# Eight-expert stages: the bias rows computed during the first blocks instead of after the last one

## The chip, the cores and the metric

The kernel runs on one core of a Trainium2 chip. The metric is the device time of one execution in microseconds, lower is better. Several executions are timed, and one further execution is recorded by the profiler. That execution has a time of its own, and its span runs from its first to its last instruction.

## The reference, cut to what matters

1,024 tokens of width 256 pass six stages, each added to a running `x`: a two-expert feed-forward, attention, the two-expert feed-forward again, an eight-expert feed-forward, a state-space mixer, the eight-expert feed-forward again. Each stage begins with a layernorm. The eight-expert stage is the one that changes. It is called twice, as the fourth and as the last stage, with the same weights:

```
logits = gelu(x @ rw1) @ rw2;  wgt, idx = top_k(softmax(logits), 2)
for e in range(8):
    Ye = gelu(x @ w1[e] + b1[e]) @ w2[e] + b2[e]
    Ce = gelu(b1[e]) @ w2[e] + b2[e]
    for k in range(2):
        mask = idx[..., k] == e
        active = any(mask)
        out = out + active * wgt[..., k] * where(mask, Ye, Ce)
x = x + 0.5 * out
```

So every token gets, besides the outputs of its own two experts, a sum of constant rows: for every active expert that it did not choose the row `Ce`, and for the chosen ones the row `b2[e]`, each weighted. This sum of constants is what is called the bias rows here: a matrix of coefficients (1,024 tokens by 16) times a matrix of 16 rows (8 of `Ce`, 8 of `b2`) by 256.

## The kernel before, in words

All activations live in SBUF as `X`, eight tiles of 128 tokens by 256. Each engine (PE for matmuls, ACT, DVE, POOL, SP for queueing transfers) runs its own instruction list in order and meets the others at semaphores. PSUM has eight banks of 512 f32 columns, `c.bank(0)` to `c.bank(7)`.

An eight-expert stage (`moe_stage` with `gated` false) goes like this. Layernorm, router and sorting give lists of token indices, so that the tokens of one expert stand in blocks of 128; there are 23 blocks (`NB`). Per block:

- POOL issues `slab_in` (line 935: 1 MB of first-layer weights of the block's expert into one of four slabs), `gather` (line 954: the block's tokens) and, once the block is done, `scatter` (line 959: its 128 output rows to `y_dram`). Its order is fixed: `slab_in(b+4)`, `gather(b+4)`, `scatter(b)`.
- PE transposes the gathered tokens (`turn_x`, line 545, bank 7), runs the first layer (`first_turned`, line 572, 48 f16 matmuls of 128 columns, banks 0 to 3) and the second layer (`second`, line 602, 24 f16 matmuls of 256 columns, bank 6). In `step_turned(b)` the order is `turn_x(b+2)`, `first_turned(b+1)`, `second(b)`.
- ACT copies the transposed tokens (line 682) and applies gelu (line 695).
- DVE makes the low halves (lines 837, 854 and 856; the last two in `half_h`) and copies the output out of PSUM (`block_y`, line 863).

Behind the last `second` stands the bias work. PE turns the coefficients `coef` (16 columns) with 8 f32 products into banks 2 and 3 (line 653). In the first of the two stages it also turns the rows `Ce` (`bias_turn`, line 1055, bank 7), to which DVE adds `b2` (`bias_add`, line 1065). ACT copies the turned coefficients to SBUF (line 740). PE multiplies them with the 16 rows, one f32 product of 256 columns for each tile of tokens (line 661, banks 0, 1, 4, 5). DVE adds half of each to `X` (line 912). In the trace each f32 product is two matmul instructions.

SP waits until all scatters have landed and then queues eight loads of 256 KB (line 985), each of which fetches a token tile's two expert rows. In `combine_first` (line 920) and `combine_second` (line 925) DVE adds them with their weights to `X`. `combine_first` of a tile waits for that tile's load and for that tile's bias row (`s_bts`). After the first of the two stages the combines run inside the mixer's layernorm, in which PE also runs unused matmuls (`keep_awake`, line 114); after the second each finished tile is stored.

Of the kernel before, what the change touches and what calls it, by code (L numbers as in the profile page):

```python
# [19 lines left out]
P = 128  # L20
T = 1024
D = 256
# [300 lines left out]
def moe_stage(c, src, E, TOPK, NB, gated, W, region, meanwhile=None, weights_act=None, weights_dve=None, weights_late=None, weights_sync=None):  # L323
# [154 lines left out]
    def pe(eng):  # L478
# [108 lines left out]
        def second(b, p, first_use=False):  # L587

            e = eng.value_load(ebi[0:1, bass.ds(b, 1)], min_val=0, max_val=E - 1)
            if not first_use:  # L590
                eng.wait_ge(*s_yo(b))
            else:
                for ready in W["second_ready"]:
                    eng.wait_ge(*ready)
            w2h, w2l = W["second"]
            i = 0
            for q in range(2):
                eng.wait_ge(*s_hl(2 * b + q + 1))
                for j in range(half):
                    at = bass.ds(e * (CF * D) + (q * half + j) * D, D)  # L600
                    for a, w in ((hTh, w2h), (hTh, w2l), (hTl, w2h)):
                        ins = eng.matmul(c.bank(6)[:, 0:D], a[:, 0 if gated else p, q * half + j, :], w[:, at],  # L602
                                         start=(i == 0), stop=(i == 3 * CF - 1))
                        i += 1
            ins.then_inc(s_y.sem, 1)

        if not gated:

            eng.wait_ge(*s_yi(1))
            W["bias_wait"](eng)  # L610
        for ready in W["block_ready"]:
            eng.wait_ge(*ready)
        def step(b, p, first_use=False, x=True):
# [4 lines left out]
                turn_x(b + 2, p)  # L618
            second(b, p, first_use)

        def step_turned(b, p, q, first_use=False, x=True):

            if x:
                turn_x(b + 2, p)
            first_turned(b + 1, 1 - p, (q + 1) % SLABS, first_use)
            second(b, p, first_use)

        turn_x(0, 0)
        turn_x(1, 1)
        if gated:  # L630
            first(0, 0)
            step(0, 0, True)
            step(1, 1)
            with eng.Fori(1, NB // 2 - 1) as i:
                step(2 * i, 0)
                step(2 * i + 1, 1)
            step(NB - 3, 0)
            step(NB - 2, 1, x=False)
            turn_h(NB - 1, 0)
        else:  # L640
            first_turned(0, 0, 0, True)
            step_turned(0, 0, 0, True)
            step_turned(1, 1, 1)
            with eng.Fori(0, NB // 4 - 1) as i:
                for j in range(2, 6):
                    step_turned(4 * i + j, j % 2, j % SLABS)
            for b in range(NB - 5, NB - 1):
                step_turned(b, b % 2, b % SLABS, x=(b < NB - 2))
        second(NB - 1, 0)
        if not gated:  # L650
            eng.wait_ge(*s_cf(1))
            for t in range(NT):
                ins = eng.matmul(c.bank(2 + t // 4)[0:2 * E, (t % 4) * P:(t % 4 + 1) * P], coef[:, t, :], c.ident[:, :],
                                 start=True, stop=True)
            ins.then_inc(s_cft.sem, 1)
            W["bias_turn"](eng)
            eng.wait_ge(*s_cfc(2))
            for ready in W["bias_done"]:
                eng.wait_ge(*ready)
            for t in range(NT):  # L660
                eng.matmul(c.bank((0, 1, 4, 5)[t // 2])[:, t % 2 * D:(t % 2 + 1) * D], coefT[:, t * P:(t + 1) * P], W["cb"], start=True, stop=True)\
                    .then_inc(s_bt.sem, 1)

    assert NB % 2 == 1 and (gated or NB % SLABS == 3)

# [1 line left out]
    def act(eng):  # L667
        L["act"](eng)
        if not gated:
            for s in range(HALVES):  # L670
                eng.wait_ge(*s_hid(s + 1))
                eng.activation(hid[:, s * BANK:(s + 1) * BANK], c.bank(s), ACT.Gelu).then_inc(s_hida.sem, 1)
        eng.wait_ge(*s_d(1))
        eng.activation(ex[:, :, :], lg[:, :, :], ACT.Exp).then_inc(s_ex.sem, 1)
        if weights_act is None:
            eng.activation(c.spent[:, 1:2], c.ln_consts[:, 0:1], ACT.Silu if gated else ACT.Gelu)
        if weights_act is not None:
            weights_act(eng)

        def block_x(b, p):  # L680
            eng.wait_ge(*s_xt(b + 1))
            eng.activation(xgh[:, p, :, :], c.bank(7)[:, 0:D].rearrange("p (k t) -> p k t", k=KD), ACT.Copy).then_inc(s_xh.sem, 1)  # L682

        def block_act(b, p):
            eng.wait_ge(*s_h1(b + 1))
            eng.activation(h[:, p, :], c.banks(0, 2), ACT.Silu).then_inc(s_a.sem, 1)  # L686

        def block_gelu(b, p, s, first_use=False):

            if not first_use:  # L690
                eng.wait_ge(*s_hl(2 * b - 2))
            for q in range(2):
                eng.wait_ge(*s_h1(2 * b + q + 1))
                for j in range(q * CF // 2, (q + 1) * CF // 2):
                    ins = eng.activation(h[:, p, j * P:(j + 1) * P], c.banks(2 * p, 2)[:, j * P:(j + 1) * P], ACT.Gelu,  # L695
                                         bias=slabs[s][:, KD * FF + j:KD * FF + j + 1])
                ins.then_inc(s_h.sem, 1)

        def block_h(b, p):
            for q in range(2):  # L700
                eng.wait_ge(*s_ht(2 * b + q + 1))
                eng.activation(hTh[:, 0, q * 4:q * 4 + 4, :], c.bank(4 + q).rearrange("p (j t) -> p j t", j=4), ACT.Copy)\
# [12 lines left out]
        def step_turned(b, p, s, first_use=False, x=True):  # L715
            if x:
                block_x(b + 2, p)
            block_gelu(b + 1, 1 - p, (s + 1) % SLABS, first_use)

        block_x(0, 0)  # L720
        block_x(1, 1)
        if gated:
            block_act(0, 0)
            for b in range(NB - 3):
                step(b, b % 2)
            step(NB - 3, 0)
            step(NB - 2, 1, x=False)
            block_h(NB - 1, 0)
        else:
            block_gelu(0, 0, 0, True)  # L730
            step_turned(0, 0, 0, True)
            step_turned(1, 1, 1)
            with eng.Fori(0, NB // 4 - 1) as i:
                for j in range(2, 6):
                    step_turned(4 * i + j, j % 2, j % SLABS)
            for b in range(NB - 5, NB - 1):
                step_turned(b, b % 2, b % SLABS, x=(b < NB - 2))
            eng.wait_ge(*s_cft(1))
            for s in range(HALVES):
                eng.activation(coefT[:, s * BANK:(s + 1) * BANK], c.bank(2 + s)[0:2 * E, :], ACT.Copy).then_inc(s_cfc.sem, 1)  # L740


    def dve(eng):
# [121 lines left out]
        def step(b, p, first_use=False, x=True):  # L865
# [7 lines left out]
            if meanwhile is not None:  # L873
                meanwhile["dve"](eng, b, True)

        def step_turned(b, p, first_use=False, x=True, y=True):
            if y:
                block_y(b - 1, 1 - p, first_use)
            if x:
                block_x(b + 2, p)  # L880
            half_h(b + 1, 1 - p, 0)
            half_h(b + 1, 1 - p, 1)
# [12 lines left out]
        else:  # L895
            half_h(0, 0, 0)
            half_h(0, 0, 1)
            step_turned(0, 0, y=False)
            step_turned(1, 1, True)
            step_turned(2, 0, True)  # L900
            with eng.Fori(1, NB // 2 - 1) as i:
                step_turned(2 * i + 1, 1)
                step_turned(2 * i + 2, 0)
            step_turned(NB - 2, 1, x=False)
            block_y(NB - 2, 1)
        block_y(NB - 1, 0)

        if not gated:
            W["bias_add"](eng)
            for t in range(NT):  # L910
                eng.wait_ge(*s_bt(t // 2 * 2 + 2))
                eng.scalar_tensor_tensor(c.X[:, t, :], c.bank((0, 1, 4, 5)[t // 2])[:, t % 2 * D:(t % 2 + 1) * D], 0.5, c.X[:, t, :],
                                         ALU.mult, ALU.add).then_inc(s_bts.sem, 1)


    def combine_first(eng, t):
# [77 lines left out]
def l1_weights(c, A, stage, w1_split, w2_split, mix_stored, w1_h, w1_l, w2_h, w2_l, rr_h, rr_l, rw2, cb, region, mem2_free, x_done, s_rows, slabs):  # L994
# [57 lines left out]

    def bias_turn(eng):
        for a in range(KD):
            ins = eng.transpose(c.bank(7)[0:E1, a * P:(a + 1) * P], cbT[:, a, :], c.ident[:, :])
        ins.then_inc(s_cr.sem, 1)

    def bias_dve(eng):
# [3 lines left out]

    def bias_add(eng):
        eng.wait_ge(*s_cr(1))
        eng.tensor_tensor(cb[0:E1, :], c.bank(7)[0:E1, 0:D], b2s, ALU.add).then_inc(s_cb.sem, 1)
# [1501 lines left out]
```

## Time and profile before

| what | value |
|---|---|
| median of 3 timed executions | 963.73 us |
| lowest and highest of them | 962.53 and 965.37 us |
| the profiled execution's own time | 959.09 us |
| its span | 957.3 us |
| PE busy (matmul) | 824.6 us, 86% of the span |
| DVE busy | 604.7 us, 63% |
| ACT busy | 429.2 us, 45% |
| mean granted clock of PE, as a share of 2.4 GHz | 0.954 |

In the profile, times are us from the span's start. The blocks of the first eight-expert stage run from about 461 to 594 us, those of the second from about 808 to 940 us. "The chain" is the work that ended last, followed back from the end of the program: what lies on it sets the time. A wait in brackets behind an instruction is how long its engine stood idle before it, and what ended that.

### The profile page before, as it was taken

The page shows a single profiled execution, that of the slowest core. Times are in us where ns is not written, and L with a number is a line of the kernel's source. Part 1 is how long each engine was busy: PE and PEld are TensorE (multiplying, and loading weights), DVE is VectorE, ACT ScalarE, POOL GpSimd, SP SyncE. Part 2 cuts the span into 40 slices and gives each one's busy share as a digit, 9 for nine tenths or more (in the row PEclk, how much of TensorE's full clock was granted, in tenths as well). Part 3 has the DMA queues.
Part 4 walks back from the last instruction along what each step waited for, and adds up shares of the span by engine and source line. Part 5 has one row for each costly group of instructions (what it writes and reads, how often), then busy time and mean ns, then how long its engine had stood idle before and what let it go on. Part 6 is the DMA issues. An engine that isn't in the chain of part 4 may idle for free.

```text
span 957.3 us, 20813 instructions
## 1 busy us (share of the span) xinstructions
PE 824.6 (86%) x7572; PEld 539.0 (56%) x7573; DVE 604.7 (63%) x1079; ACT 429.2 (45%) x995; POOL 355.4 (37%) x419
## 2 busy tenths in 40 slices
PE   3399979689987799998899999897899867999994
PEld 2166644233333346664789998444344434999993
DVE  5656656689953446646555664786798646556655
ACT  6445543257773434435344543475111162445441
POOL 2312134141110302123445542326997533455530
PEclk9999999799998799988999999899999998999997
DMA  8335645231124324422986661200000014666644
GB/s 291 118 96 170 179 156 182 71 100 33 28 101 171 103 64 160 150 63 69 334 301 236 227 236 61 88 0 1 0 1 0 1 44 167 234 236 228 236 153 149
DMA packets 45909, 125.35 MB, mean 131 GB/s; under 512 B 10201, under 2 KB 23466, under 8 KB 39822
## 3 DMA queue, kind: packets, MB, share of 16 engines
q0 software_dynamic: 13872, 69.54, 20.7%
q1 hardware_dynamic: 25834, 47.78, 15.2%
q10 hardware_dynamic: 6132, 7.05, 2.3%
q8 instruction: 48, 0.79, 0.3%
q14 instruction: 23, 0.19, 0.1%
HBM read 97.28 MB, written 26.71 MB: 130 GB/s over the span
## 4 chain that ended last, share of the span: by engine, by line
PE 59%; DVE 13%; POOL 8%; ACT 7%; DMA 6%; issue 6%; ACTq 0%; SPq 0%; POOLq 0%; DVEq 0%
PE psum L602 17%; PE psum L572 12%; PE psum L558 9%; PE psum L1411 4%; POOL mem L2222 3%; DMA mem<-xn_dram,mem 2%; DVE mem L1549 2%; POOL mem L2218 2%; PE psum L1383 2%; PE psum L545 2%; PE psum L114 1%; PE psum L1357 1%; PE psum L583 1%; ACT mem L182 1%; POOL ln_rstd L164 1%
## 5 line engine op out<-in xcount | busy, mean ns | idle before, releaser
L602 PE MATMUL psum<-mem 128*128 x1536 | 178.9, 273 | 3.7 <-DVE mem L847 2.5
L602 PEld LDWEIGHTS psum<-mem 128*128 128x128 f16 x1536 | 146.0, 98 | 24.1 <-issue 4.7
L959 POOL DMA_INDIRECT y_dram<-mem x64 | 66.0, 1032 | 187.1 <-DVE mem L863 187.1
L572 PE MATMUL psum<-mem 128*128 128x128 f16 x2208 | 130.8, 220 | 0.0
L695 ACT ACTIVATE mem<-psum,mem 128x128 f32<-128x128 f32 x368 | 104.9, 368 | 56.3 <-PE psum L572 54.9
L572 PEld LDWEIGHTS psum<-mem 128*128 128x128 f16 x2208 | 126.7, 98 | 0.8
L954 POOL DMA_INDIRECT mem<-xn_dram,mem x64 | 65.3, 1021 | 103.4 <-PE psum L545 78.7
L558 PE MATMUL psum<-mem 128*128 x432 | 102.4, 397 | 0.4 <-issue 0.3
L1549 DVE TENSOR_REDUCE mem<-psum 128x2 f32<-128x1024 f32 (+2 forms) x96 | 87.6, 945 | 15.2 <-PE psum L1357 9.9
L1497 ACT ACTIVATE mem<-psum 128x512 f32<-128x512 f32 (+1 forms) x160 | 79.9, 552 | 37.5 <-PE psum L1391 21.4
L854 DVE CAST mem<-mem 128x512 f16<-128x512 f32 x92 | 45.7, 496 | 79.2 <-ACT mem L695 78.1
L114 PE MATMUL psum<-ones 128*128 128x512 f16 x268 | 84.6, 434 | 0.6 <-issue 0.6
L682 ACT ACTIVATE mem<-psum 128x256 f16<-128x256 f32 x64 | 24.5, 382 | 117.6 <-PE psum L545 117.6
L558 PEld LDWEIGHTS psum<-mem 128*128 128x128 f16 x432 | 43.8, 101 | 52.6 <-issue 9.1
L856 DVE TENSOR_TENSOR mem<-mem 128x512 f16<-128x512 f32 x92 | 65.7, 714 | 3.2
L1929 PE MATMUL psum<-mem 128*128 128x512 f32 x112 | 55.1, 617 | 10.9 <-DVE psum L2144 10.7
L935 POOL DMA_INDIRECT mem<-w_rows,mem x46 | 45.2, 982 | 41.0 <-DVE mem L781 23.4
L198 PE MATMUL psum<-ident,mem 128*128 128x128 f32 x96 | 24.3, 341 | 32.1 <-ACT mem L182 31.9
L249 DVE TENSOR_TENSOR mem<-stage,mem 128x1024 f16<-128x1024 f32 (+1 forms) x36 | 41.5, 1177 | 11.6 <-ACT mem L272 9.9
L842 DVE TENSOR_TENSOR mem<-mem,psum 128x1024 f32<-128x1024 f32 x18 | 22.0, 1221 | 42.4 <-ACT mem L686 42.3
L1411 PE MATMUL psum<-mem 128*17 128x384 f32 (+3 forms) x480 | 48.0, 439 | 0.7
L863 DVE COPY mem<-psum 128x256 f32<-128x256 f32 x64 | 27.1, 424 | 30.5 <-PE psum L602 30.5
(257 smaller groups left out, 1328.6 us busy)
## 6 DMA issues: line engine op xcount, KB each, us to landing
stage<-in_w SPq DMA_DIRECT2D x32, 512.0 KB, 3.9
w_rows<-mem SPq DMA_DIRECT2D x8, 1024.0 KB, 8.8
xn_dram<-mem ACTq DMA_DIRECT2D x32, 128.0 KB, 1.7
mem<-y_dram SPq DMA_DIRECT2D x16, 256.0 KB, 4.9
mem<-in_w_gate SPq DMA_DIRECT2D x4, 512.0 KB, 7.2
mem<-in_w_up SPq DMA_DIRECT2D x4, 512.0 KB, 10.4
mem<-in_w_down SPq DMA_DIRECT2D x4, 512.0 KB, 13.7
mem<-y_dram SPq DMA_DIRECT2D x16, 128.0 KB, 2.8
```

The lines of the kernel that those rows point to most:

```text
L114: eng.matmul(c.bank(bank), c.ones16[:, :], wide, start=True, stop=True)
L558: ins = eng.matmul(c.bank(2 * m + s), a[:, p, k, :], w[:, at], start=(i == 0), stop=(i == 3 * KD - 1))
L572: ins = eng.matmul(c.bank(2 * p + j // half)[:, j % half * P:(j % half + 1) * P], mats[q][:, l, k, j * P:(j + 1) * P], x[:, p, k, :], star ...
L602: ins = eng.matmul(c.bank(6)[:, 0:D], a[:, 0 if gated else p, q * half + j, :], w[:, at], start=(i == 0), stop=(i == 3 * CF - 1))
L695: ins = eng.activation(h[:, p, j * P:(j + 1) * P], c.banks(2 * p, 2)[:, j * P:(j + 1) * P], ACT.Gelu, bias=slabs[s][:, KD * FF + j:KD * FF ...
L856: eng.tensor_tensor(hTl[:, p, part, :], gelu, hTh[:, p, part, :], ALU.subtract).then_inc(s_hl.sem, 1)
L954: eng.indirect_dma_start(xg[:, b % 2, :], None, c.xn_dram[:, :], bass.IndirectOffsetOnAxis(ap=idx[:, b:b + 1], axis=0)).then_inc(s_xg[b % ...
L959: eng.indirect_dma_start(c.y_dram[:, :], bass.IndirectOffsetOnAxis(ap=yidx[:, b:b + 1], axis=0), yo[:, b % 2, :], None).then_inc(s_ys[b % ...
L1411: ins = eng.matmul(c.bank(7)[at:at + VW, a - y * BANK:a - y * BANK + w], va[:, k, 2 * p + j, :], pt[:, g % RING, 2 * y + j, off:off + w], ...
L1497: eng.activation(pt[:, g % RING, 2 * y + j, 0:w], c.bank(4 + at % 3)[:, 0:w], ACT.Exp, scale=DK ** -0.5).then_inc(s_ex.sem, 1)
L1549: eng.tensor_reduce(out, c.banks(2 * (i % 2), 2).rearrange("p (j q) -> p j q", j=2)[:, :, 0:w], AX.X, ALU.max)\
L1929: ins = eng.matmul(acc(2 * p + j), gm[:, i % RING, j, :], xw[:, i % RING, j, :], start=False, stop=True, skip_group_check=True)
```

## The change

The work is the same; its place in the instruction lists differs, and some banks with it.

- PE: the turning of the coefficients stands in `step_turned(0)`, between `first_turned(1)` and `second(0)`, and writes banks 4 and 5. The products for tiles 0 to 3 stand in `step_turned(1)`, between `first_turned(2)` and `second(1)`; those for tiles 4 to 7 behind `second(1)`, with a wait for DVE's first four additions, since they use banks 4 and 5 again. `bias_turn` stands ahead of block 0's `turn_x` and uses bank 6, so the first two `second` wait for `bias_add`.
- ACT: the two copies stand between the work of step 0 and of step 1.
- DVE: `bias_add` stands behind block 0's `half_h`; the additions to `X` for tiles 0 to 3 behind `step_turned(1)`, those for tiles 4 to 7 behind `step_turned(2)`.

```diff
@@ second @@
                 for ready in W["second_ready"]:
                     eng.wait_ge(*ready)
+                if not gated:
+                    eng.wait_ge(*W["bias_done"][0])
@@ pe @@
             W["bias_wait"](eng)
+            W["bias_turn"](eng)
...
+        def turn_coef():
+            eng.wait_ge(*s_cf(1))
+            for t in range(NT):
+                ins = eng.matmul(c.bank(4 + t // 4)[0:2 * E, (t % 4) * P:(t % 4 + 1) * P], coef[:, t, :], c.ident[:, :],
+                                 start=True, stop=True)
+            ins.then_inc(s_cft.sem, 1)
+
+        def bias_rows(r):
+            if r:
+                eng.wait_ge(*s_bts(NT // 2))
+            else:
+                eng.wait_ge(*s_cfc(2))
+                for ready in W["bias_done"]:
+                    eng.wait_ge(*ready)
+            for t in range(r * NT // 2, (r + 1) * NT // 2):
+                eng.matmul(c.bank(4 + t // 2 % 2)[:, t % 2 * D:(t % 2 + 1) * D], coefT[:, t * P:(t + 1) * P], W["cb"], start=True, stop=True)\
+                    .then_inc(s_bt.sem, 1)
...
-            step_turned(0, 0, 0, True)
-            step_turned(1, 1, 1)
+            step_turned(0, 0, 0, True, between=turn_coef)
+            step_turned(1, 1, 1, between=lambda: bias_rows(0))
+            bias_rows(1)
...
         second(NB - 1, 0)
-        if not gated:
-            eng.wait_ge(*s_cf(1))
-            for t in range(NT):
-                ins = eng.matmul(c.bank(2 + t // 4)[0:2 * E, (t % 4) * P:(t % 4 + 1) * P], coef[:, t, :], c.ident[:, :],
-                                 start=True, stop=True)
-            ins.then_inc(s_cft.sem, 1)
-            W["bias_turn"](eng)
-            eng.wait_ge(*s_cfc(2))
...
@@ act @@
             step_turned(0, 0, 0, True)
+            eng.wait_ge(*s_cft(1))
+            for s in range(HALVES):
+                eng.activation(coefT[:, s * BANK:(s + 1) * BANK], c.bank(4 + s)[0:2 * E, :], ACT.Copy).then_inc(s_cfc.sem, 1)
             step_turned(1, 1, 1)
...
@@ dve @@
             half_h(0, 0, 1)
+            W["bias_add"](eng)
             step_turned(0, 0, y=False)
             step_turned(1, 1, True)
+            bias_rows(0)
             step_turned(2, 0, True)
+            bias_rows(1)
...
         block_y(NB - 1, 0)
-
-        if not gated:
-            W["bias_add"](eng)
-            for t in range(NT):
-                eng.wait_ge(*s_bt(t // 2 * 2 + 2))
```

## Rows read from the trace of the kernel before

**Rows 1.** The page's chain, by line, with shares of the span.
```profile
PE psum L602 17%; PE psum L572 12%; PE psum L558 9%; PE psum L1411 4%; POOL mem L2222 3%; DMA mem<-xn_dram,mem 2%; DVE mem L1549 2%; POOL mem L2218 2%; PE psum L1383 2%; PE psum L545 2%; PE psum L114 1%; PE psum L1357 1%; PE psum L583 1%; ACT mem L182 1%; POOL ln_rstd L164 1%
```

**Rows 2.** Windows: stretch, length, busy PE, PEld, DVE, ACT, POOL, clock, DMA share, GB/s.
```profile
490.00:590.50 100.50, 100.50 (x1336) 93.89 (x1334) 59.03 (x108) 47.55 (x161) 46.46 (x48) 1.00 0.58 205
820.00:936.70 116.70, 116.70 (x1554) 109.26 (x1551) 68.16 (x125) 55.54 (x188) 55.41 (x57) 1.00 0.60 208
```

**Rows 3.** Chain, two neighbouring blocks of the second stage: start, length, what.
```profile
920.64 2.68 PE psum L572 x48
...
926.16 2.68 PE psum L572 x48
```

**Rows 4.** Chain behind the last block of the first stage.
```profile
594.00 1.86 PE psum L653 x16
...
595.89 1.07 ACT mem L740 x2
...
597.00 5.28 PE psum L661 x16
...
603.06 0.40 DVE X L920
```

**Rows 5.** Chain behind the last block of the second stage.
```profile
940.17 1.86 PE psum L653 x16
...
943.17 3.73 PE psum L661 x16
...
947.68 0.40 DVE X L920
```

**Rows 6.** Timeline behind the first stage's last block: scatter, turned rows, first load.
```profile
594.74 0.97 POOL L959 DMA_INDIRECT y_dram<-mem  x1 [2.44 <-DVE mem L863]
595.78 0.38 PE L1055 MATMUL psum<-ident,mem 128*8 128x128 f32 x2
597.17 4.91 SPq L985 DMA_DIRECT2D mem<-y_dram  x8
```

**Rows 7.** Line 985 in the first eight-expert stage: from issue to landing.
```profile
DMA to landing us min/median/max: 4.3/4.7/5.0
```

**Rows 8.** Line 985 in the second eight-expert stage: from issue to landing.
```profile
DMA to landing us min/median/max: 4.8/5.1/5.5
```

**Rows 9.** Timeline behind the second stage's last block: loads, additions, last tile's first combine.
```profile
943.37 3.94 SPq L985 DMA_DIRECT2D mem<-y_dram  x8
944.34 3.35 DVE L912 SCALAR_TENSOR_TENSOR X<-psum,X 128x256 f32<-128x256 f32 x8 [3.70 <-PE psum L661]
954.01 0.48 DVE L920 SCALAR_TENSOR_TENSOR X<-mem,X 128x256 f32<-128x256 f32 x1
```

**Rows 10.** Windows behind the first stage's last block (columns as in rows 2).
```profile
597.17:599.50 2.33, 2.33 (x10) 1.94 (x11) 1.23 (x4) 0.00 (x0) 0.00 (x0) 0.90 0.40 115
...
599.00:605.50 6.50, 6.50 (x16) 3.20 (x16) 4.60 (x13) 0.20 (x1) 0.42 (x2) 0.50 0.94 292
```

**Rows 11.** Timeline of PE: `turn_x(4)` and `turn_x(5)` of the first stage.
```profile
477.57 0.43 PE L545 MATMUL psum<-ident,mem 128*128 128x128 f32 x2 [0.81 <-DMA mem<-xn_dram,mem]
...
484.79 0.43 PE L545 MATMUL psum<-ident,mem 128*128 128x128 f32 x2 [1.38 <-DMA mem<-xn_dram,mem]
```

**Rows 12.** Chain ahead of the second of these waits: block 5's tokens.
```profile
474.57 10.10 DMA mem<-xn_dram,mem
```

**Rows 13.** Windows behind the second two-expert stage (columns as in rows 2).
```profile
424.90:435.00 10.10, 9.84 (x99) 5.33 (x96) 6.40 (x20) 5.16 (x17) 3.93 (x10) 0.50 0.46 141
```

**Rows 14.** Chain and timeline: first combine and last layernorm piece behind both two-expert stages.
```profile
132.34 0.50 DVE X L920
...
146.94 0.44 DVE XTl L156
...
425.93 0.48 DVE L920 SCALAR_TENSOR_TENSOR X<-mem,X 128x256 f32<-128x256 f32 x1 [4.39 <-DMA mem<-y_dram]
...
441.22 0.43 DVE XTl L156
```

More of the change, by code:

```diff
@@ L619, in step, with step_turned @@
             second(b, p, first_use)
-        def step_turned(b, p, q, first_use=False, x=True):
+        def turn_coef():
[14 more added lines that the diff above has]
+                    .then_inc(s_bt.sem, 1)
+        def step_turned(b, p, q, first_use=False, x=True, between=None):
             if x:
@@ L625, in step_turned @@
             first_turned(b + 1, 1 - p, (q + 1) % SLABS, first_use)
+            if between is not None:
+                between()
             second(b, p, first_use)
@@ L649, in pe @@
         second(NB - 1, 0)
-        if not gated:
-            eng.wait_ge(*s_cf(1))
-            for t in range(NT):
-                ins = eng.matmul(c.bank(2 + t // 4)[0:2 * E, (t % 4) * P:(t % 4 + 1) * P], coef[:, t, :], c.ident[:, :],
-                                 start=True, stop=True)
-            ins.then_inc(s_cft.sem, 1)
-            W["bias_turn"](eng)
-            eng.wait_ge(*s_cfc(2))
-            for ready in W["bias_done"]:
-                eng.wait_ge(*ready)
-            for t in range(NT):
-                eng.matmul(c.bank((0, 1, 4, 5)[t // 2])[:, t % 2 * D:(t % 2 + 1) * D], coefT[:, t * P:(t + 1) * P], W["cb"], start=True, stop=True)\
-                    .then_inc(s_bt.sem, 1)
     assert NB % 2 == 1 and (gated or NB % SLABS == 3)
@@ L737, in act @@
                 step_turned(b, b % 2, b % SLABS, x=(b < NB - 2))
-            eng.wait_ge(*s_cft(1))
-            for s in range(HALVES):
-                eng.activation(coefT[:, s * BANK:(s + 1) * BANK], c.bank(2 + s)[0:2 * E, :], ACT.Copy).then_inc(s_cfc.sem, 1)
     def dve(eng):
@@ L874, in step, with bias_rows @@
                 meanwhile["dve"](eng, b, True)
+        def bias_rows(r):
+            for t in range(r * NT // 2, (r + 1) * NT // 2):
+                eng.wait_ge(*s_bt(t // 2 * 2 + 2))
+                eng.scalar_tensor_tensor(c.X[:, t, :], c.bank(4 + t // 2 % 2)[:, t % 2 * D:(t % 2 + 1) * D], 0.5, c.X[:, t, :],
+                                         ALU.mult, ALU.add).then_inc(s_bts.sem, 1)
         def step_turned(b, p, first_use=False, x=True, y=True):
@@ L906, in dve @@
         block_y(NB - 1, 0)
-        if not gated:
-            W["bias_add"](eng)
-            for t in range(NT):
-                eng.wait_ge(*s_bt(t // 2 * 2 + 2))
-                eng.scalar_tensor_tensor(c.X[:, t, :], c.bank((0, 1, 4, 5)[t // 2])[:, t % 2 * D:(t % 2 + 1) * D], 0.5, c.X[:, t, :],
-                                         ALU.mult, ALU.add).then_inc(s_bts.sem, 1)
     def combine_first(eng, t):
@@ L1054, in bias_turn @@
         for a in range(KD):
-            ins = eng.transpose(c.bank(7)[0:E1, a * P:(a + 1) * P], cbT[:, a, :], c.ident[:, :])
+            ins = eng.transpose(c.bank(6)[0:E1, a * P:(a + 1) * P], cbT[:, a, :], c.ident[:, :])
         ins.then_inc(s_cr.sem, 1)
@@ L1064, in bias_add @@
         eng.wait_ge(*s_cr(1))
-        eng.tensor_tensor(cb[0:E1, :], c.bank(7)[0:E1, 0:D], b2s, ALU.add).then_inc(s_cb.sem, 1)
+        eng.tensor_tensor(cb[0:E1, :], c.bank(6)[0:E1, 0:D], b2s, ALU.add).then_inc(s_cb.sem, 1)
     stage_ = dict(sync=load_cb, act=bias_act, dve=bias_halves, load_w2=load_w2)
```

## The prediction, as it was put on record

> **What bounds the kernel now.** I read the page's chain first. By line, the two feed-forward layers of the expert stages lead it: line 602 has 17% and line 572 has 12% [rows 1]. So in the eight-expert stages the question is always what PE does. The windows over the steady blocks answer it: in the first stage PE is busy for 100.50 of 100.50 us, in the second for 116.70 of 116.70 us, at a clock of 1.00, which is the upper of its two levels (2.4 GHz) [rows 2]. DVE is busy for 68.16 and ACT for 55.54 of the same 116.70 us, POOL for 55.41, and the DMA share is 0.60. The chain of two neighbouring blocks shows a period of 926.16 - 920.64 = 5.52 us [rows 3], all of it PE. A matmul put among these blocks moves everything behind it by its full length; an instruction of DVE or ACT does not.
>
> Then I read what stands behind the last block. In the first stage the last `second` ends at 594.00. Turning the coefficients takes 1.86 us, ACT's copies 1.07, the products 5.28, and the first combine starts at 603.06 [rows 4]: a tail of 9.1 us. In the second stage it is 947.68 - 940.17 = 7.5 us, with 1.86 for the turning and 3.73 for the products [rows 5]. The products took longer in the first stage because the granted clock was 0.50 from 599.0 on [rows 10].
>
> The reader should now see what else runs in this tail. The last scatter is issued at 594.74, and SP can queue the loads of the expert rows only when it has landed, at 597.17 [rows 6]. These loads took 4.3 to 5.0 us to land [rows 7], in the second stage 4.8 to 5.5 [rows 8]. So the bias work runs beside a round trip through memory that the combines need as well. It has a cover where it stands; only what sticks out behind the round trip can be won.
>
> **The change, part by part.**
>
> *PE, added to the blocks.* The turning is 16 instructions, 1.86 us [rows 4, 5]. The products are 16 instructions, 3.73 us at the full clock [rows 5]; the blocks run at 1.00, so this is the price, not the 5.28. Together 5.59 us in each stage. In the first stage `bias_turn` moves ahead of `turn_x(0)`: two instructions, 0.38 us modelled [rows 6], 0.2 if they overlap; I take 0.3. It starts when PE's unused matmuls end, where nothing hides it.
>
> *PE, what it fills.* In the first stage PE waits twice for gathered tokens soon after the place of the new work: 0.81 us at `turn_x(4)` and 1.38 us at `turn_x(5)` [rows 11], 2.2 in all. PE now comes later by 5.9 us, so these waits shrink. The gather of block 5 was issued at 474.57 and landed 10.10 us later [rows 12]. In POOL's queue it stands behind `scatter(0)`, which waits for `second(0)`, now later by 1.86 + 0.3. So it lands by 484.67 + 2.2 = 486.8. PE came to `turn_x(5)` at 484.79 - 1.38 = 483.4; less the first wait and with the new work it comes at 483.4 - 0.8 + 5.9 = 488.5. The wait is gone with 1.7 us to spare. In the second stage PE has no wait behind `turn_x(2)` and before the last block, so nothing is filled [rows 2]. PE grows by 5.9 - 2.2 = 3.7 us in the first stage and by 5.6 us in the second. Bounds: in the first, 3.6 with the 0.2, and 5.2 if gather 5 slips as far as PE does and only 0.8 us is filled.
>
> *ACT.* Two copies, 1.07 us, between gelu of block 1 and the tokens of block 3. ACT is idle for more than half of each block [rows 2], and PE runs `second(0)` meanwhile. No cost; without the cover 1.07 us.
>
> *DVE.* Eight additions take 3.35 us [rows 9], four of them 1.7, plus one `bias_add` of about 0.4. DVE is idle for 2.3 of 5.5 us per block [rows 2]. The tightest place is the wait of the second half of the products for the first four additions. These stand behind `half_h(2)`, which ends about 2.4 us behind `first_turned(2)`; so they end at about 4.1. PE comes there after 1.87 of products and 2.6 of `second(1)`, at 4.5. It fits by 0.4 us. Bound: 0 to 1.0 us if it misses. The additions of tiles 4 to 7 push `block_y(2)` back by about 1.4 us. What waits for that is `scatter(2)` on POOL, with the slab and the gather behind it that are needed two blocks later, and `second(3)`, about 1 us after the new end. No cost. The new wait of the first two `second` for `bias_add` is met: DVE is there while PE still turns coefficients.
>
> *The tail of the first stage.* The combines now wait for the loads alone. The first is queued 3.2 us behind the last matmul, as before. The rows do not give its own landing. By 599.50 the engines had moved 115 GB/s x 2.33 us = 0.27 MB [rows 10], one tile's 256 KB, so not before 599.5; by the least landing of the row, 4.3 us, it is 601.5 [rows 7]. I take 600.4, since in the second stage the first tile was there by 947.60 at the latest, at most 4.2 us behind its issue, with nothing waiting. Gain 603.0 - 600.4 = 2.6 us, bounds 1.5 and 3.5.
>
> The Trainium skill ("DMA: Bandwidth & Descriptors", Anatomy of one DMA) gives about 2.0 us fixed plus the bytes over 436 GB/s, an estimate of 2.6 us for 256 KB. By it the tile lands at 599.8 and the gain is 3.2 us, so the sum would be 0.6 us lower. The trace's own 4.3 to 5.0 us for loads queued together do not agree.
>
> From this I take off a loss. PE will have done its 14 unused matmuls long before the first normalized tile and be idle for some microseconds, so the layernorm's transposes probably begin at the lower level (0.50, 1.2 GHz). Behind the second two-expert stage the same code ran at 0.50 [rows 13], and from first combine to the last piece it took 441.65 - 425.93 = 15.7 us, against 147.38 - 132.34 = 15.0 at the full clock behind the first [rows 14]. I take 0.5 us, bounds 0 and 0.7. Net gain 2.1 us, from 0.8 to 3.5.
>
> *The tail of the second stage.* The first load is queued at 943.37 [rows 9]. Its combine can start at some 946.1 instead of 947.6. But the last load is queued at 946.8 and lands 5.5 us later [rows 8], at 952.3, while its combine stood at 954.01 [rows 9]. So no more than 1.7 us can be won. I take 1.4, bounds 0.6 and 1.7, as the stores now share the transfers a little earlier.
>
> *Sum.* First stage 3.7 - 2.1 = +1.6 us; second stage 5.6 - 1.4 = +4.2 us; together +5.8 us, or 959.09 + 5.8 = 964.9 for the profiled execution. The median of the timed runs stands 4.6 us above that execution, and none of the terms is near it in kind, so I add to the median: 963.73 + 5.8 = 969.5 us. With all bounds low: 3.6 - 3.5 + 5.6 - 1.7 = +4.0, 967.7. High: 5.2 + 1.0 - 0.8 + 5.6 + 1.0 - 0.6 = +11.4, 975.1; with half of the high surprises, 972.3.
>
> **Rivals.**
>
> *The extra matmuls find cover (faster).* If the opening of both stages were paced by transfers, PE could take the bias work in its waits. For it: PE does wait for gathers at `turn_x(4)` and `turn_x(5)` [rows 11], and a transfer of tokens took 10.10 us there [rows 12]. Against it: those waits are 2.2 us in one stage and none behind the new work in the other. With all 11.5 us covered the time is 963.7 - 2.1 - 1.4 = 960.2 us. It decides only when 8.7 of the 11.5 us are covered beyond the 2.2. Chance 5%.
>
> *A wash.* The tails give their full bounds (5.2 us), and 1.1 us or more of the matmuls is hidden as well, for instance in a wait for tokens that the profiled execution happened not to show in the second stage. Time 963.7 + 2.9 or less, say 966. Chance 11%.
>
> *The clock falls in the first blocks (slower still).* The products use 16 rows of the array. In the tail the clock fell to 0.50 during them, behind a pause of PE of 0.8 us, and stayed there until 605.5 [rows 10]; in the second stage it held through them. Were it to fall for 6.5 us among the blocks, half of that, 3.3 us, is lost each time: 973 to 976 us. Against it: there is no pause, and dense f16 matmuls stand on both sides. Chance 10%.
>
> *The forecast*, 967.5 to 973: 74%.
>
> **Numbers.** A measurement of this kernel tells about 0.3%, 2.9 us, from no change. Faster comes from the first rival alone, 0.05; within 0.3% from the wash, 0.11; slower from the rest, 0.84. The range reaches from the edge of the wash to the first cases of the fallen clock: 966.0 to 974.0 us. The forecast's own range is 967.5 to 973.
>
> **What would show it.** In the profile after: lines 653 and 661 at about 1.9, 1.9 and 1.9 us in the first three blocks, at clock 1.00; no wait for tokens at `turn_x(4)` and `turn_x(5)` of the first stage; the last `second` of the first stage 3.7 us later against the stage's start, of the second 5.6; the first combine 6.4 us behind the last matmul in the first stage and 5.9 in the second, waiting for line 985's load. The prediction is wrong if `second` ends later by clearly less than these amounts, or if the first combine starts earlier than 5.5 us behind the last matmul; and too low if PE waits for DVE ahead of the second half of the products, or the mixer's first matmuls run at 0.50.

## The result, and the profile after

In 20 executions of each kernel the median went from 962.66 to 966.66 us. The ratio is 1.0038, with a 95% interval of 1.0021 to 1.0054: the change makes the kernel slower by 3.7 us (2.0 to 5.2). The forecast was slower by 5.8 us. A ratio, here and below, uses only executions at their usual speed (it leaves out, for instance, one of e3's that took 1,237.2 us) and is not the quotient of the two medians, which can differ from it by a microsecond or more.

The recorded execution after took 966.88 us, its span is 965.1 us and its mean granted clock 0.942. Between the two recorded executions lie 7.8 us of span, more than the timed medians show. So I split both traces at the same four places: the start of the sorting's one-hot operation ahead of the blocks, the end of the last `second` of each eight-expert stage, and the end. Stretches in us, each the difference of two starts or ends in the timeline:

| stretch | before | after | difference | forecast |
|---|---|---|---|---|
| start to the first stage's sorting (code unchanged) | 452.95 | 455.45 | +2.5 | 0 |
| sorting to last `second`, first stage | 141.05 | 144.70 | +3.65 | +3.7 |
| last `second` to first combine | 8.98 | 6.06 | -2.9 | -2.6 |
| last `second` to the mixer's first matmuls (holds the row above) | 25.68 | 22.78 | -2.9 | -2.1 |
| the mixer up to the second stage's sorting | 180.47 | 180.46 | 0.0 | 0 |
| sorting to last `second`, second stage | 140.02 | 145.79 | +5.8 | +5.6 |
| last `second` to first combine | 7.43 | 5.95 | -1.5 | -1.6 |
| last `second` to the end (holds the row above) | 17.13 | 15.92 | -1.2 | -1.4 |

The 2.5 us of the first row lie in code that is the same in both kernels, and are the spread from one execution to the next. What is left is 3.65 - 2.9 + 5.8 - 1.2 = +5.3 us in these two executions.

The timeline of PE in the first three blocks after, first stage (start, length, engine, line, operation, tiles and shapes, count):

```profile
471.17 1.92 PE L628 MATMUL psum<-ident,mem 128*16 128x128 f32 x16
473.02 2.79 PE L604 MATMUL psum<-mem 128*128 x24
475.65 0.38 PE L545 MATMUL psum<-ident,mem 128*128 128x128 f32 x2
475.87 2.84 PE L572 MATMUL psum<-mem 128*128 128x128 f16 x48
478.64 1.99 PE L641 MATMUL psum<-mem 16*128 16x256 f32 x8
480.56 2.79 PE L604 MATMUL psum<-mem 128*128 x24
483.28 1.99 PE L641 MATMUL psum<-mem 16*128 16x256 f32 x8
485.20 0.44 PE L545 MATMUL psum<-ident,mem 128*128 128x128 f32 x2
...
490.91 0.38 PE L545 MATMUL psum<-ident,mem 128*128 128x128 f32 x2
```

Line 628 is the turning and line 641 the products. There is no bracket behind any row, so PE waits for nothing. The rows at 485.20 and 490.91 are `turn_x(4)` and `turn_x(5)`, which had waited 0.81 and 1.38 us [rows 11]. The chain, which takes off the overlap of neighbours, gives the net price (start, length, what):

```profile
471.24 1.85 PE psum L628 x16
...
478.71 1.92 PE psum L641 x8
...
483.35 1.92 PE psum L641 x8
...
820.42 1.85 PE psum L628 x16
...
827.89 1.92 PE psum L641 x8
...
832.54 1.92 PE psum L641 x8
```

That is 5.7 us in each stage, where the prediction had 5.59. DVE's timeline shows the tightest place:

```profile
480.44 0.69 DVE L869 TENSOR_TENSOR mem<-mem 128x512 f16<-128x512 f32 x1
481.06 1.41 DVE L893 SCALAR_TENSOR_TENSOR X<-psum,X 128x256 f32<-128x256 f32 x4
483.39 0.42 DVE L876 COPY mem<-psum 128x256 f32<-128x256 f32 x1 [0.93 <-PE psum L604]
```

The first four additions end at 482.47 and the second half of the products starts at 483.28, 0.8 us later: PE doesn't wait. Windows over the openings and over a tail (stretch, length, busy PE, PEld, DVE, ACT, POOL, clock, DMA share, GB/s):

```profile
474.00:480.00 6.00, 6.00 (x73) 5.56 (x72) 1.90 (x5) 2.75 (x10) 2.84 (x3) 1.00 1.06 416
480.00:486.00 6.00, 6.00 (x47) 4.65 (x47) 2.85 (x8) 0.32 (x1) 1.76 (x3) 1.00 1.00 402
...
826.00:836.00 10.00, 10.00 (x100) 8.39 (x98) 4.57 (x11) 2.67 (x9) 4.77 (x6) 1.00 0.41 146
```

```profile
605.00:608.00 3.00, 0.00 (x0) 0.00 (x0) 1.72 (x5) 0.00 (x0) 0.00 (x0) 1.00 0.96 308
608.00:610.00 2.00, 0.00 (x0) 0.00 (x0) 1.93 (x8) 0.80 (x3) 1.35 (x3) 0.58 0.98 336
610.00:612.00 2.00, 1.65 (x5) 0.93 (x6) 1.79 (x6) 1.64 (x6) 1.50 (x3) 0.50 0.55 194
```

The clock stays at 1.00 (2.4 GHz) through the 16-row products in both openings. In the tail PE is idle, and the layernorm's first transposes run at 0.50 (1.2 GHz). The chain behind the first stage's last block, which answers to [rows 4]:

```profile
597.33 2.82 PE psum L604 x24
...
600.87 2.41 DMA y_dram<-mem
603.30 2.88 DMA mem<-y_dram
606.21 0.49 DVE X L936
...
622.93 1.56 PE psum L1873 x48
```

The bias work is gone from it. The scatter's round trip has taken its place: 2.41 us for the last scatter and 2.88 for the first load.

### The profile page after: what moved, and what is told of

It is laid out like the page before. It is cut to its first block, busy times and chain, and to the rows that moved or that the text cites. A ratio compares the mean times of both kernels' runs of the same rounds, so it can differ in the third digit from the quotient of the medians.

```text
span 965.1 us, 20815 instructions
## 1 busy us (share of the span) xinstructions
PE 830.6 (86%) x7572; PEld 542.3 (56%) x7573; DVE 602.5 (62%) x1079; ACT 429.8 (45%) x995; POOL 355.5 (37%) x419
## 4 chain that ended last, share of the span: by engine, by line
PE 60%; DVE 13%; POOL 8%; ACT 7%; issue 6%; DMA 5%; SPq 0%; ACTq 0%; POOLq 0%; DVEq 0%
PE psum L604 17%; PE psum L572 13%; PE psum L558 9%; PE psum L1427 4%; DVE mem L1565 3%; POOL mem L2238 2%; POOL mem L2234 2%; PE psum L545 2%; PE psum L1373 2%; PE psum L1399 2%; PE psum L114 1%; PE psum L583 1%; DMA mem<-xn_dram,mem 1%; ACT mem L182 1%; DMA mem<-y_dram 1%
## 5 line engine op out<-in xcount | busy, mean ns | idle before, releaser
L114 PE MATMUL psum<-ones 128*128 128x512 f16 x268 | 88.1, 448 | 0.6 <-issue 0.6
```

Source lines behind the costliest of these rows:

```text
L114: eng.matmul(c.bank(bank), c.ones16[:, :], wide, start=True, stop=True)
```

## The experiments

Each edit is shown against the kernel named. "Ratio" is the timed one to the kernel before, with its 95% interval, measured beside it on the same chip.

**1. Only the turning moved (e1).** Products and additions go back behind the last block; the turning and `bias_turn` stay where the change put them.

```diff
-            step_turned(1, 1, 1, between=lambda: bias_rows(0))
-            bias_rows(1)
+            step_turned(1, 1, 1)
...
         second(NB - 1, 0)
+        if not gated:
+            bias_rows(0)
+            bias_rows(1)
```

> The changed kernel with one part undone: the products and the additions to X stand behind the last block again; the turning of the coefficients, ACT's copies and bias_turn stay early. Theory A (PE's time in the blocks is paid in full, and the tail hides what fits under the scatter and the loads): the blocks of the first stage grow by 1.9 + 0.3 less the two waits for tokens of 2.2, so by 0 to 0.5 us; those of the second by 1.9. The products now start right behind the last matmul and end 3.8 us later, ahead of the first load's landing at 6.0, so both tails stay as short as in the changed kernel: 3.0 and 1.2 us shorter than before. Sum -2 us, ratio to the kernel before about 0.998. Rival B (the blocks hide the extra matmuls at least in part): as much as the changed kernel or slightly better, -4 us only if the turning is hidden too. Rival C (the loss comes from something other than the products, such as the two waits for bias_add or bias_turn ahead of block 0): still slower than before, ratio over 1.002.

Measured: 960.65 against 961.74 us, ratio 0.9982 (0.9961 to 1.0003). In its trace the first combine starts 6.2 and 6.0 us behind the last `second`, as soon as in the kernel after, though all the products run there. The time cannot be told from that of the kernel before, but it is clear of the kernel after (1.0021 to 1.0054). So the products, two thirds of what the change put into the blocks, bought nothing: moving the turning alone frees the whole of what stuck out of the round trip.

**2. The turning one place earlier (e2).** Against e1, it stands ahead of `turn_x(2)`, where PE had waited for tokens.

```diff
             first_turned(0, 0, 0, True)
-            step_turned(0, 0, 0, True, between=turn_coef)
+            turn_coef()
+            step_turned(0, 0, 0, True)
```

> As the kernel with the products behind the last block, but the coefficients are turned one step earlier, ahead of turn_x(2), where PE of the second stage waits 1.4 us for gathered tokens. Theory A: the second stage's blocks grow by 1.86 - 1.45 = 0.4 us instead of 1.9, the first stage's by 0 to 0.5, tails 3.0 and 1.2 us shorter than before: about -3.5 us, ratio 0.996. Rival: the wait for tokens moves with PE, because the gather waits for PE's earlier transposes; then it equals the kernel with the later turning, ratio 0.998.

Measured: 959.55 us, ratio 0.9967 (0.9949 to 0.9986), faster than before by 3.2 us. The second stage's blocks took 140.42 us, against 140.02 before and 141.71 in e1: here the turning lies almost wholly in a wait. The first stage's blocks did not gain by it in these recordings (142.96 us, against 142.25 in e1 and 141.05 before), and the timed ratios of e1 and e2 overlap.

**3. Without the bias work (e3).** Against the kernel after: turning, copies, products and additions are gone from PE, ACT and DVE, as is `bias_turn`.

```diff
-            step_turned(0, 0, 0, True, between=turn_coef)
-            step_turned(1, 1, 1, between=lambda: bias_rows(0))
-            bias_rows(1)
+            step_turned(0, 0, 0, True)
+            step_turned(1, 1, 1)
```

> Leaves the bias rows out: no turning, no products, no additions, no bias_turn and bias_add (the sums for the rows Ce are still made). It shows the least that any placing could reach. Theory A: the first combine stands 6.0 us behind the last matmul in both stages, as in the changed kernel, since the scatter and the loads set it; blocks as before the change: -3.0 - 1.2 = -4.2 us, ratio 0.9956. Rival: if the bias work in the tail had not been covered by the round trip, leaving it out would give the whole 9.1 and 7.5 us less a few tenths; then ratio under 0.99.

Measured: 959.65 us, ratio 0.9955 (0.9928 to 0.9982). That is 4.3 us below before, for the whole of the work, and no more than e2 can be told apart from: what the bias work still costs in e2 is within the error. Its first combines start 6.05 and 6.08 us behind the last `second`, so this is what the round trip takes by itself. Its trace also shows what the prediction had too small (PE's timeline, then windows):

```profile
483.95 0.69 PE L545 MATMUL psum<-ident,mem 128*128 128x128 f32 x2 [3.55 <-DMA mem<-xn_dram,mem]
484.43 5.33 PE L572 MATMUL psum<-mem 128*128 128x128 f16 x48
```

```profile
483.90:489.00 5.10, 5.05 (x45) 5.00 (x46) 0.98 (x3) 1.52 (x5) 0.94 (x1) 0.50 1.03 364
```

Without the work in the opening PE waits 3.55 us for the tokens of block 4, and then the clock is 0.50 and the first layer takes 5.33 instead of 2.84 us. So in this recording the first stage's blocks take 144.80 us with less work in them than before, where they took 141.05.

**4. The same PE time in the blocks, the tail as it was (e4).** Against the kernel before: 8 unused turnings and 8 unused products at the places of the change.

```diff
-            step_turned(0, 0, 0, True)
-            step_turned(1, 1, 1)
+            step_turned(0, 0, 0, True, between=extra_turn)
+            step_turned(1, 1, 1, between=lambda: extra_rows(0))
+            extra_rows(1)
```

> The kernel before, with extra matmuls whose results nobody reads: the same 16 and 16 instructions per stage, of the same shapes, at the places where the changed kernel has them; the tail keeps its own bias work. It prices PE's time in the blocks alone. Theory A: first stage +5.6 less the two waits of 2.2 = +3.4, second stage +5.6: +9.0 us, ratio 1.0093. Rival B (the blocks hide part of it): under +5 us. Rival D (the clock falls for products of 16 rows): over +12 us.

Measured: 970.86 us, ratio 1.0090 (1.0062 to 1.0118), +8.7 us. The blocks take 144.67 and 144.63 us in its trace, +3.6 and +4.6 (the wait of 1.45 us that the kernel before had at `turn_x(2)` of its second stage is not in this recording). The first combines start 8.97 and 8.25 us behind the last `second`, against 8.98 and 7.43 before; why the second tail is 0.8 us longer with the same code is told in the next section. PE's time in the blocks is paid, and the change's gain is in the tails alone. The clock held in both openings:

```profile
470.00:482.00 12.00, 12.00 (x132) 10.45 (x130) 6.27 (x12) 4.62 (x17) 5.00 (x5) 1.00 1.03 390
482.00:494.00 12.00, 12.00 (x145) 10.61 (x144) 4.39 (x9) 4.49 (x16) 4.87 (x5) 1.00 0.69 262
...
822.00:834.00 12.00, 12.00 (x123) 10.28 (x121) 5.45 (x10) 3.79 (x13) 4.01 (x5) 1.00 0.60 211
```

**5. The work among the late blocks (e5).** Against the kernel after: the same instructions, but in steps 18 and 19 of 22, where PE never waits.

```diff
-            step_turned(0, 0, 0, True, between=turn_coef)
-            step_turned(1, 1, 1, between=lambda: bias_rows(0))
-            bias_rows(1)
+            step_turned(0, 0, 0, True)
+            step_turned(1, 1, 1)
...
+                step_turned(b, b % 2, b % SLABS, x=(b < NB - 2),
+                            between={NB - 5: turn_coef, NB - 4: lambda: bias_rows(0)}.get(b))
+                if b == NB - 4:
+                    bias_rows(1)
```

> The changed kernel with the bias work moved from the first blocks to late ones: the turning in step 18, the products in step 19 and behind it, ACT's and DVE's parts beside them. The tails are those of the changed kernel. Theory A: the extra matmuls no longer fill PE's waits for tokens in the opening of the first stage, so it is slower than the changed kernel by these waits: 2.2 us by the profiled execution of before; more if other executions wait longer, as the one without bias rows did (3.6 us, and a fallen clock behind it). Ratio to the kernel before 1.006 to 1.009. Rival (the place among the blocks does not matter): as the changed kernel, 1.004.

Measured: 970.56 us, ratio 1.0080 (1.0054 to 1.0106). Against before it is +7.7 us where the kernel after has +3.7, so the place in the opening is worth about 4 us by the two ratios, with an error of some 3 us from their intervals. PE's timeline and a window show them:

```profile
480.87 0.69 PE L545 MATMUL psum<-ident,mem 128*128 128x128 f32 x2 [3.70 <-DMA mem<-xn_dram,mem]
481.35 5.33 PE L572 MATMUL psum<-mem 128*128 128x128 f16 x48
```

```profile
481.00:486.00 5.00, 5.00 (x46) 4.92 (x47) 1.06 (x3) 1.52 (x5) 0.95 (x1) 0.50 1.01 365
```

**6 and 7. The waits taken away at their source (e6, e7).** The windows of the opening show the transfers full (DMA share 1.00 to 1.06, 402 to 416 GB/s). Besides slabs and gathers, SP fetches the mixer's 3.4 MB of weights there, released by `begun`. In both kernels this now starts with block 10.

```diff
-                ready=..., begun=s_h1(1), idle_bank=3, ...)
+                ready=..., begun=s_h1(1) if gated else s_h1(2 * 10 + 1), idle_bank=3, ...)
```

On the kernel before (e6):

> The kernel before with one transfer moved: the loads of the mixer's matrices, 3.4 MB on SP's queue, start with block 10 of the first eight-expert stage instead of block 0. Theory A (PE's waits for tokens in that opening come from these loads, and are what the changed kernel fills): the waits at turn_x(4) and turn_x(5) are gone, 2.2 us less than the profiled execution had, and up to 4 us in the mean of the timed ones: ratio 0.996 to 0.998. Rival (the tokens are late for another reason, POOL's order): no change, ratio 1.000.

On the kernel after (e7):

> The changed kernel with the same transfer moved. Theory A: it has no waits left to lose, so it stays where the changed kernel is, ratio 1.004 to the kernel before; against the kernel before with the transfer moved the change then costs its full sum without the fill: 5.9 + 5.6 less 3.0 and 1.2 of the tails = 7.3 us, a ratio of about 1.0076 between the two. Rival (the fill is worth nothing): both kernels gain alike.

Measured: before 960.97 us, ratio 0.9971 (0.9946 to 0.9995); after 968.56 us, ratio 1.0060 (1.0036 to 1.0083). The second over the first is 1.0089, or +8.6 us; their medians differ by 7.6 us. The first-stage waits at `turn_x(4)` and `turn_x(5)` are gone from the trace of e6. But a new one stands where the moved loads now run:

```profile
534.75 0.43 PE L545 MATMUL psum<-ident,mem 128*128 128x128 f32 x2 [1.51 <-DMA mem<-xn_dram,mem]
```

e7 and e8 have it as well (1.53 and 1.48 us), so it drops out between e6 and e7. In e6 the blocks of the first stage take 140.23 us, 0.8 less than before and not 2.2. The work in the opening has nothing to fill in either kernel now, and the prediction's own terms then give 5.9 - 2.1 + 5.6 - 1.4 = +8.0 us, near both readings. What the change itself costs less than that is the fill: 8.6 - 3.7 = 4.9 us by the ratios, 7.6 - 4.0 = 3.6 us by the medians.

**8. The best of it (e8).** Against e2: `bias_turn` and two of the turnings stand between `turn_x(0)` and `turn_x(1)`, the other six ahead of `turn_x(2)`, and the mixer's weights come late.

```diff
         turn_x(0, 0)
+        if not gated:
+            W["bias_turn"](eng)
+            turn_coef(range(2))
         turn_x(1, 1)
...
-            turn_coef()
+            turn_coef(range(2, NT))
```

> The combination that the runs point to: products and additions behind the last block; bias_turn and the first two of the eight turning products between turn_x(0) and turn_x(1), where PE waits 1.0 us in both stages; the other six ahead of turn_x(2); the mixer's loads from block 10 on. Theory A: first stage: 1.4 us of matmuls without cover (the waits for tokens are gone with the loads), but these waits' 2.2 to 4 us gained; second stage: nothing added, since 1.4 fits into the wait ahead of turn_x(2); tails 3.0 and 1.2 shorter: -5 to -7 us, ratio 0.993 to 0.995. Rival: if the waits for tokens do not go, it is -4 us, 0.996.

Measured: 958.57 against 962.94 us, ratio 0.9951 (0.9927 to 0.9975). It beats both kernels: 4.7 us below before by the ratio, 8.4 below after. The blocks take 141.72 and 139.91 us, the first combine starts 5.96 and 6.01 us behind them. That it beats e2 as well is not shown: the intervals overlap.

**9. How much the round trip still covers (e9).** Against e2: 8 further unused products behind the last block, ahead of the real ones.

```diff
         if not gated:
+            for t in range(NT):
+                eng.matmul(c.bank((0, 1, 4, 5)[t // 2])[:, t % 2 * D:(t % 2 + 1) * D], coefT[:, t * P:(t + 1) * P], W["cb"], start=True, stop=True)
             bias_rows(0)
             bias_rows(1)
```

> As the kernel that turns the coefficients ahead of turn_x(2), but behind the last block PE makes the eight products twice, 16 more instructions or 3.7 us, the first time unused. It measures how much work the scatter and the loads still cover. Theory A: the first set ends 3.8 us behind the last matmul, the second 7.5 us, DVE's last addition about 8 us; the first combine moves from 6.0 to about 8 us behind the last matmul in both stages, so only 2 of the added 3.7 us show: +4 us to the single products, ratio to the kernel before 1.000 to 1.001. Rival (matmuls in the tail are paid like those in the blocks): +7.4 us, ratio 1.004.

Measured: 973.27 against 967.69 us, ratio 1.0046 (1.0009 to 1.0082). These runs were on another chip, on which the kernel before itself ranged from 959.49 to 982.26 us, so the ratio says little; the tails in the trace say more. Their chains:

```profile
600.67 3.65 PE psum L679 x16
604.32 4.96 PE psum L639 x16
```

```profile
954.08 3.65 PE psum L679 x16
957.73 6.76 PE psum L639 x16
```

and windows of the second tail:

```profile
957.00:959.00 2.00, 2.00 (x8) 1.63 (x7) 0.00 (x0) 0.00 (x0) 0.00 (x0) 0.67 0.30 55
959.00:961.00 2.00, 2.00 (x6) 1.53 (x6) 0.76 (x2) 0.00 (x0) 0.00 (x0) 0.50 0.88 289
```

The unused products (line 679) take 3.65 us, but the real ones behind them (line 639) 4.96 and 6.76 instead of 3.73: the clock fell to 0.50 during them, as the windows show for the second tail. The first combine starts 9.3 and 11.1 us behind the last `second`, where I had expected about 8. So one set of products fits below the round trip of 6.0 us and a second one does not. The ratio is that of the rival (1.004), but for another reason: by the traces the size was missed because of the clock. A single set in the second tail took 3.72 us in e1, 4.08 in e2 and 4.65 in e8, and it stayed below the round trip each time.

**10. e8 without the moved prefetch (e10).**

```diff
-                begun=s_h1(1) if gated else s_h1(2 * 10 + 1)
+                begun=s_h1(1)
```

> The combination without the moved transfer: products and additions behind the last block, bias_turn and two turning products between turn_x(0) and turn_x(1), six ahead of turn_x(2). Theory A: nothing of the turning is paid in the second stage, and the waits for tokens in the first stage's opening stay, filled by 1.4 us: about -4 us, ratio 0.996. Rival: the moved transfer gave most of the gain of the full combination; then this one is at 0.998 or above.

Measured on the same chip as e9: 965.62 us, ratio 0.9994 (0.9955 to 1.0033). Inconclusive: the expected 0.996 lies just inside the interval, and no change does as well.

**11. The kernel before once more (e11).**

> The kernel before once more, for a second profile of it. Theory A (its waits for tokens in the opening of the first stage differ between executions, and the recorded one had short ones): the waits at turn_x(4) and turn_x(5) add up to another number than 2.2 us, more likely above it, and the granted clock may fall behind a long one. Rival: they are 2.2 us again, and the fill that late placing loses has another cause.

Measured: one execution, 971.61 us, span 969.8. PE's timeline, and a window behind the wait:

```profile
481.61 0.69 PE L545 MATMUL psum<-ident,mem 128*128 128x128 f32 x2 [2.97 <-DMA mem<-xn_dram,mem]
```

```profile
481.50:486.50 5.00, 4.89 (x55) 4.67 (x56) 0.94 (x3) 1.92 (x7) 2.51 (x3) 0.70 1.02 403
```

The unchanged kernel waits 2.97 us here, once, and its clock falls behind the wait; in the execution that the prediction read it was 0.81 and 1.38 us at a clock of 1.00. At 0.70 for 5.0 us some 1.5 us of PE's time are lost, so wait and clock cost about 4.5 us together in this execution. Its blocks of the first stage take 143.79 us, 2.7 more than in the recording that the prediction read. The second tail differs too: its products take 5.63 us and the first combine starts 9.34 us behind the last `second`, against 3.72 and 7.43.

## Why the prediction was right, and which terms were off

The sign and the mechanism were right: PE's work is paid among the blocks, and only what outlasts the round trip is won in the tails. The size was at the edge. 966.66 us lies 0.7 us inside the range of 966.0 to 974.0 and below the forecast's own 967.5 to 973; the kernel before came out at 962.66 us instead of 963.73, and the measured +3.7 is what the prediction had with all bounds low (+4.0). The terms that were off all made the sum too large. Step by step:

- *PE added to the blocks.* Forecast 5.59 us per stage; 5.7 in the trace. Shown to be paid by e4 (+8.7 us with the bias work of the tails left in place).
- *The fill of PE's waits: probably the largest miss.* "So these waits shrink", 2.2 us, was read from one execution, and I took it for the typical one. The waits did vanish, as the step said, and between the two recorded executions the term even fits (3.65 against 3.7). By the timed runs the fill is worth 4.9 or 3.6 us (e7 over e6, less the change) and 4.0 (e5 against after), but only 5.6 + 5.6 - 8.7 = 2.5 by e4, which fills the same waits. Each of these has an error of 2 to 4 us by the intervals, so they do not exclude 2.2. The traces show what can make it larger: in e3, e5 and e11 the wait is 3.0 to 3.7 us in one piece, the clock falls behind it, and that costs up to 2.5 us more (5.33 against 2.84 us in line 572). The prediction had a fall of the clock as a rival that makes the change slower; it didn't see that the kernel before can run into it. With 4.0 in place of 2.2 the sum is +4.0 us, but since these figures come from timed differences, the change's own among them, that is no second proof.
- *The second half of the products waits for DVE.* Forecast: fits by 0.4 us. It fits by 0.8.
- *The first tail.* The first load was issued 3.15 us behind the last matmul (forecast 3.2) and landed 2.88 us later (forecast 3.2). The Trainium skill's sum ("DMA: Bandwidth & Descriptors", Anatomy of one DMA), which that section fits to transfers issued by POOL while these are queued by SP, gives 2.6 us as an estimate and was as near on the other side. The 4.3 to 5.0 us of [rows 7] were misread: for each stage that view has landings for the last four of the eight loads only, so its least value was no bound for the first load. The cold layernorm was forecast to cost 0.5 us. It did run at 0.50, but from first combine to the mixer's matmuls it took 622.93 - 606.21 = 16.7 us, against 619.68 - 603.06 = 16.6 before: 0.1 us. By the chain that stretch waits for DVE, ACT and POOL, and hardly for PE. Net 2.9 us, forecast 2.1.
- *The second tail: another single reading.* Forecast 1.4 us, 1.2 between the two recorded executions. The chain shows a late load, as forecast, but it is the fourth, not the last; from then on the combines run one behind the other. It lands 4.34 us from its issue at 953.80:

```profile
953.80 4.34 DMA mem<-y_dram
958.17 0.49 DVE X L936
```

But the tail before has the same code in e4, e11 and e6, and there its products took longer than the 3.72 us of the recording that the prediction read (in this order, and a window of e6):

```profile
953.81 4.54 PE L675 MATMUL psum<-mem 16*128 16x256 f32 x16 [1.15 <-ACT mem L754]
...
953.88 5.63 PE L661 MATMUL psum<-mem 16*128 16x256 f32 x16 [1.15 <-ACT mem L740]
...
942.91 6.04 PE L661 MATMUL psum<-mem 16*128 16x256 f32 x16 [1.15 <-ACT mem L740]
```

```profile
945.00:947.00 2.00, 2.00 (x6) 1.57 (x5) 0.76 (x2) 0.00 (x0) 0.00 (x0) 0.50 0.97 308
```

The clock fell to 0.50 during them. From the last `second` to the end it is 17.13 us in the recording before, 17.79 in e4, 18.92 in e11 and 19.29 in e6. In the eight recordings in which at most one set of products stands there and the turning does not (after, e1, e2, e3, e5, e7, e8, e10) it is 15.68 to 16.61. The means differ by 2.0 us, more than the 1.7 that the prediction called the most that can be won.
- *The rivals.* That the matmuls find cover is shown wrong by e4 and e5. The fallen clock in the first blocks did not come: 1.00 in both openings. The wash is near in its result (its own words give +2.9 us or less), but not for its reasons: the tails gave 4.1 us in the recorded pair, not 5.2, and nothing was hidden in the second stage, where the blocks grew by 5.8 us.

What the change missed is shown by e1 and e3. Of the bias work behind the last block, only what stuck out of the 6.0 us round trip was on the path: 2.9 and 1.5 us in the recorded pair. The turning alone (1.85 us, and the copies and the pause that come with it) is all that had to go for that; the products went from a covered place to one where each microsecond is paid.

What stays open: how the 1.6 us between the +5.3 of the two recorded executions and the timed +3.7 divide between the fill and the second tail, since only single executions are recorded; whether e10 gains without the moved prefetch; and whether e8 loses its wait of 1.48 us if the mixer's loads are spread over more blocks.

## What to carry to other kernels

Before moving work out of a tail, find what else runs beside it: only the part that outlasts the round trip through memory can be won, so move the smallest piece that brings the rest below it. A place between dense matmuls is paid in full, one ahead of a wait for a transfer is nearly free (e1 to e2: the same turning, one position earlier, took 1.3 us off the second stage's blocks). A wait or a tail read from one execution is a sample: where transfers run at their limit or PE runs only small products, look at a second trace before its size enters a sum, and ask what the clock does there. A transfer that is moved out of the way can make a wait where it goes (1.51 us in e6).

## What the runs showed of the hardware

A wait of PE for tokens of 3.55 or 3.70 us was followed by some 5 us at the lower clock level, with dense f16 matmuls from its end on. Behind the one of 2.97 us the clock was 0.70 over 5 us; behind those of 0.81 and 1.38 us it stayed at 1.00.

The clock also fell while PE was busy throughout: in e6 it was 0.50 at 945 to 947 us, with the f32 products of 16 rows running for 2.00 of 2.00 us behind a pause of 1.15 us. Among dense f16 matmuls the same products ran at 1.00 (826 to 836 us in the kernel after).

The spread between executions does not come from the waits for data alone. In e11 one block of the second stage took 9.37 us from one `turn_x` to the next instead of some 5.5, with no wait for a tile (PE's timeline, then windows):

```profile
839.66 0.41 PE L602 MATMUL psum<-mem 128*128 x2
840.68 0.38 PE L602 MATMUL psum<-mem 128*128 x2 [0.61 <-issue]
841.41 0.27 PE L602 MATMUL psum<-mem 128*128 x1 [0.35 <-issue]
842.13 3.54 PE L602 MATMUL psum<-mem 128*128 x19 [0.45 <-issue]
```

```profile
840.00:842.00 2.00, 0.72 (x4) 0.19 (x2) 0.00 (x0) 0.00 (x0) 0.95 (x1) 1.00 0.90 283
842.00:844.00 2.00, 1.87 (x13) 1.48 (x14) 0.62 (x2) 1.83 (x8) 0.00 (x0) 0.72 0.99 354
844.00:846.00 2.00, 2.00 (x12) 1.56 (x10) 1.71 (x4) 0.34 (x2) 0.00 (x0) 0.50 0.24 90
```

The matmuls of one layer came with gaps between them at a DMA share of 0.90 to 0.99, and the clock fell behind that too. Why they came late was not tried.
